# Dump rows stored one image sooner and three blocks long, block limits computed behind the last slots, class rows copied during the last block

## What is computed

```python
def reference(x, cls_tok, ...):
    h = tok_mixer(x)                       # exp(k)*v weighted by exp(w_bias), gate, out_w, layernorm
    h = concat([cls_tok, h], axis=1)       # the class token's row heads every image: 257 rows
    h = h + gated_recurrence(layernorm(h)) # W_r, W_i, W_in, scan over the sequence, W_out
    z = layernorm(h)
    shared = gelu(z @ Wfc_s + bfc_s) @ Wproj_s + bproj_s
    top2, gate = top_k(softmax(z @ Wr), 2) # gates normalised over the two
    routed = sum over e of gate_e * (gelu(z @ Wfc[e] + bfc[e]) @ Wproj[e] + bproj[e])
    return h + shared + routed             # (16, 257, 256)
```

## Time and profile before

| | |
|---|---|
| Median of three runs | 982.86 us |
| The profiled execution: time, span | 984.09 us, 982.0 us |
| PE busy | 921.2 us, 94% |
| DVE, ACT, POOL busy | 700.6, 482.3, 394.2 us |
| Mean granted TensorE clock | 0.98 of full |
| Moved by DMA | 89.11 MB, mean 91 GB/s |

### The profile page before, as it was taken

How to read it: one execution, slowest core, us unless ns; L and a number is a source line. 1 busy time by engine, 2 the same in 40 slices (tenths; PEclk the granted TensorE clock), 3 DMA queues, 4 the chain that set the end, 5 groups by cost and what they waited for, 6 DMA issues and landing times.

```text
span 982.0 us, 21456 instructions
## 1 busy us (share of the span) xinstructions
PE 921.2 (94%) x6825; PEld 858.8 (87%) x6825; DVE 700.6 (71%) x2093; ACT 482.3 (49%) x1146; POOL 394.2 (40%) x475
## 2 busy tenths in 40 slices
PE   7887999999999999999995999999999999999995
PEld 5665988888888888887985999999999999999995
DVE  3578788999999999999886464645646565654643
ACT  2123455555455555454341555555555555555553
POOL 6442233444333444315553334343533434342322
PEclk9898899999999999999997999999999999999998
DMA  9600001111101111101662728282642827473222
GB/s 257 187 22 23 30 31 50 54 54 54 46 18 43 54 54 54 54 1 40 199 220 69 220 44 220 43 221 43 161 107 44 219 44 190 77 205 60 44 43 33
DMA packets 50536, 89.11 MB, mean 91 GB/s; under 512 B 6733, under 2 KB 31199, under 8 KB 50498
## 3 DMA queue, kind: packets, MB, share of 16 engines
q0 software_dynamic: 31440, 58.52, 24.8%
q1 hardware_dynamic: 19058, 30.11, 10.8%
HBM read 59.28 MB, written 29.09 MB: 90 GB/s over the span
## 4 chain that ended last, share of the span: by engine, by line
PE 36%; DVE 27%; issue 23%; POOL 9%; ACT 3%; POOLq 1%; DVEq 1%; DMA 0%; ACTq 0%; SPq 0%
PE ps_nd L810 11%; PE ps_proj L794 5%; POOL out L755 5%; DVE rden L1996 4%; PE ps_ri L794 3%; DVE GL L1810 3%; PE ps_ip L960 3%; PE ps_ip L794 3%; PE ps_h L975 3%; DVE w2l L2228 2%; DVE st L1827 2%; PE ps_proj L889 1%; PE ps_proj L891 1%; PE ps_proj L894 1%; DVE h L1833 1%
## 5 line engine op out<-in xcount | busy, mean ns | idle before, releaser
L1810 DVE TENSOR_TENSOR GL<-g_act,GH 128x256 fp32r<-128x256 f32 (+1 forms) x416 | 174.6, 426 | 168.1 <-ACT GH L1440 152.9
L810 PE MATMUL ps_nd<-w2h,GH 128*128 128x256 f32 x832 | 242.5, 291 | 6.1 <-DVE Y L1999 4.8
L1435 ACT ACTIVATE g_act<-ps_proj,fcb 128x256 f32<-128x256 f32 (+1 forms) x272 | 129.1, 475 | 234.9 <-PE ps_proj L794 226.3
L810 PE MATMUL ps_nd<-w2h,GL 128*128 128x256 f32 x832 | 234.2, 281 | 0.0
L810 PE MATMUL ps_nd<-w2l,GH 128*128 128x256 f32 x832 | 233.3, 280 | 0.0
L810 PEld LDWEIGHTS ps_nd<-w2h,GH 128*128 128x128 f32 x832 | 156.6, 188 | 12.2 <-DVE Y L1999 5.0
L1440 ACT CAST GH<-g_act 128x256 fp32r<-128x256 f32 (+1 forms) x416 | 161.3, 400 | 1.2
L810 PEld LDWEIGHTS ps_nd<-w2l,GH 128*128 128x128 f32 x832 | 157.4, 189 | 0.0
L810 PEld LDWEIGHTS ps_nd<-w2h,GL 128*128 128x128 f32 x832 | 156.7, 188 | 0.0
L794 PE MATMUL ps_proj<-xh,w1h 128*128 128x256 f32 (+1 forms) x544 | 122.6, 307 | 12.6 <-DVE E L1989 8.9
L755 POOL DMA_INDIRECT out<-yb,rows_to x72 | 115.5, 1605 | 16.8 <-issue 13.2
(11 more groups left out here) (281 smaller groups left out, 1932.1 us busy)
## 6 DMA issues: line engine op xcount, KB each, us to landing
R<-v_rows SPq DMA_DIRECT2D x37, 260.0 KB
w1h<-fc_w POOLq DMA_DIRECT2D x9, 1024.0 KB
w2h<-pj_w POOLq DMA_DIRECT2D x9, 1024.0 KB
stage<-fc_w POOLq DMA_DIRECT2D x9, 1024.0 KB
stage<-pj_w POOLq DMA_DIRECT2D x9, 1024.0 KB
x<-x SPq DMA_DIRECT2D x28, 256.0 KB, 4.0
v_rows<-tail_rows SPq DMA_DIRECT2D x8, 520.0 KB
out<-yb SPq DMA_DIRECT2D x16, 256.0 KB
```

The source lines that it names most:

```text
L810: last = pe.matmul(banks[a], g[:, j, a * P:(a + 1) * P], w[i][:, j, :], start=(j == 0 and q == 0), stop=(j == HT - 1 and q == 2))
L1435: act.activation(g_act[:, j % G_SLOTS, 0:width], banks[j % len(banks)][:, 0:width], ACT.Gelu_apprx_tanh, bias=fcb[i][:, j:j + 1]).then_inc ...
L1810: dve.tensor_tensor(GL[:, j, 0:width], g_act[:, j % G_SLOTS, 0:width], GH[:, j, 0:width].bitcast(F32), ALU.subtract).then_inc(gl_done, 1)
```

## The change

- The counts for the tails are taken after image 13 (`NIMG - 3`), not 14, and the eight stores stand ahead of the base store of image 13 in SyncE's list. Each is three blocks long. POOL waits for them ahead of the scatters of image 14, not 15.
- The counting code of `experts_vector` is cut in two. `block_bounds`, up to `bounds_ready`, goes behind `slots_out(18, 0)`; `block_places`, up to `where_ready`, ahead of `base_sum(18, 0)`.
- SyncE copies the class rows when the adds of the last block but one have landed, and no longer waits for the last R. POOL waits for the last adds itself, as its last step.
- `next_low_first` and `next_low_second` become four calls of `next_low`; the instructions and their order stay.

```diff
                 for e in range(NE):
                     end = sp.value_load(ends_i[0:1, e:e + 1], min_val=e * LIST,
-                                        max_val=e * LIST + TOK - BLK)
-                    sp.dma_start(v_rows[bass.ds(end, 2 * BLK), :]
-                                 .rearrange("(b p a) m -> p b a m", b=2, a=2),
-                                 tail_rows[:].unsqueeze(1).to_broadcast([P, 2, 2, W])
+                                        max_val=e * LIST + TOK - 2 * BLK)
+                    sp.dma_start(v_rows[bass.ds(end, 3 * BLK), :]
+                                 .rearrange("(b p a) m -> p b a m", b=3, a=2),
+                                 tail_rows[:].unsqueeze(1).to_broadcast([P, 3, 2, W])
                                  ).then_inc(tails_stored, 16)
...
             base_out(16, 0)
+            tails(17, 1)
             base_out(17, 1)
-            tails(18, 0)
             base_out(18, 0)
...
-            sp.wait_ge(added, end * 32 + 32)
-            sp.wait_ge(rows_loaded, end * 16 + 16)
+            sp.wait_ge(added, end * 32)
             first_rows = out[0:NIMG * SEQ, :].rearrange("(n s) m -> n s m", s=SEQ)[:, 0, :]
...
-                    if isinstance(n, int) and n == NIMG - 1:
+                    if isinstance(n, int) and n == NIMG - 2:
                         pool.wait_ge(tails_stored, 16 * NE)
...
-            expert(NE, 0, *limits(NE), 0)
+            first, end = limits(NE)
+            expert(NE, 0, first, end, 0)
+            pool_wait(pool, added, end * 32 + 32).then_inc(carried, 1)
...
-                    if isinstance(n, int) and n == NIMG - 2:
-                        dve.wait_ge(run_ready, NIMG)
+                    if isinstance(n, int) and n == NIMG - 3:
+                        dve.wait_ge(run_ready, NIMG - 1)
                         dve.tensor_copy(ends_i[:], run[:]).then_inc(ends_ready, 1)
...
             slots_out(18, 0)
+            block_bounds(18, 0)
             low(18, 0, 1)
...
             v_norm(18, 0)
+            block_places(18, 0)
             base_sum(18, 0)
```

More of the change, by code:

```diff
@@ L668, in next_weights, with next_low @@
                 load_stage(pool, 1)
[L670 to L676, removed]
+            def next_low(t, par, q):
+                split_low(pool, 1, 1, q)
             def step(t, par):
@@ L735, in mixer_pool @@
             rstd_h(18, 0)
-            next_low_first(17, 1)
+            next_low(17, 1, 0)
+            next_low(17, 1, 1)
             rows_out(18, 0)
             affine(18, 0)
-            next_low_second(18, 0)
+            next_low(18, 0, 2)
+            next_low(18, 0, 3)
             rstd_u(18, 0)
@@ L2240, in constant, with count_chain, block_bounds, block_places @@
                 constants()
+            counted = [0]
+            def count_chain(instruction):
+                counted[0] += 1
+                instruction.then_inc(count_dve, 1)
+                dve.wait_ge(count_dve, counted[0])
+            def block_bounds(t, par):
+                chain = count_chain
+                dve.wait_ge(run_ready, NIMG + 1)
+                chain(dve.tensor_tensor(cnt["size"][:], run[:], list_f[:], ALU.subtract))
+                chain(dve.tensor_scalar(cnt_i[:], cnt["size"][:], float(BLK - 1), None, ALU.add))
+                chain(dve.tensor_scalar(cnt_s[:], cnt_i[:], BLK.bit_length() - 1, None,
+                                        ALU.arith_shift_right))
+                chain(dve.tensor_copy(cnt["n"][:], cnt_s[:]))
+                chain(dve.tensor_scalar(cnt["blocks"][:], cnt["n"][:], float(MIN_BLKS), None, ALU.max))
+                chain(dve.tensor_tensor_scan(cnt["end"][:], ones_pp[:, 0:NE], cnt["blocks"][:],
+                                             0.0, ALU.mult, ALU.add))
+                dve.memset(bounds[:, 0:1], 0)
+                dve.memset(lasts[:, 0:1], 0)
+                chain(dve.tensor_scalar(lasts[:, 1:NE + 1], cnt["end"][:], -1.0, None, ALU.add))
+                dve.tensor_copy(bounds[:, 1:NE + 1], cnt["end"][:]).then_inc(bounds_ready, 1)
+            def block_places(t, par):
+                chain = count_chain
+                dve.tensor_scalar(cnt["skip"][:], cnt["blocks"][:], -1.0, float(LIST_BLKS),
+                                  ALU.mult, ALU.add)
+                dve.tensor_copy(hop[:, NE - 1, :], block_f[:])
+                chain(dve.memset(carrier["count"][:], 0.0))
+                for e in range(NE - 1):
+                    last = dve.tensor_scalar(hop[:, e, :], block_f[:], cnt["end"][:, e:e + 1],
+                                             cnt["skip"][:, e:e + 1], ALU.is_ge, ALU.mult)
+                chain(last)
+                chain(dve.tensor_reduce(where[:], hop[:].rearrange("p e b -> p b e"), AX.X, ALU.add))
+                dve.tensor_copy(where_i[:], where[:]).then_inc(where_ready, 1)
             def cls_scan(t, par):
```

28 lines of the change are left out of this document (removed).

## The result

The changed kernel is slower. Its median is 988.94 us (986.83 to 991.55) against 982.83 (979.64 to 985.98) of the kernel before, eleven runs each: ratio 1.0059, 95% interval 1.0046 to 1.0073. The forecast was 981.3 with a range to 985.3. The profiled run is one of 988.94 us, span 987.3, clock 0.978. The profiled run of the kernel before, 984.09 us, lay 1.3 above its median, so the two traces show 4.9 us of the difference (5.3 on the span); the rest of the 6.1 between the medians stands in no trace.

The account below looks back on a forecast made before the run. TensorE was taken to set the pace except between mixer and experts (late residual sum, counts, limit loads) and at the end (class-row copy). Middle +0.3 and end -1.9 gave -1.6 us: 981.3 us, range 977.8 to 985.3.

Parts of the forecast that it names:

- The bytes of the tails: Dump-row stores before the last scatters: 6.39 MB, with 0.96 MB in their way, take 20.2 us and land at 512.4.
- the exchange of 3.3 against 3.1: DVE, image 14: base sum loses 3.3 us waiting for its store; the residual sum, no longer beside splits, returns 3.1.
- The first hold: Mixer's end: a GL part due at 517.9 is caught by POOL's first pair of splits until 522.6.
- The end, -1.9: Program end: copying class rows during the last block ends the span at about 980.1 instead of 982.0, 1.9 us less.
- a tail like that of now, 0.4: Program end: after POOL sees the last add and a 0.2 us operation, only 0.4 us remain.
- The bound of 0: Program end: no gain if the end of the program waits for something other than the class-row copy.
- the rest of the chain follow as it did: Mixer's end: behind the caught GL part, 9.7 us as before, so TensorE ends at 532.3.
- the middle: Passage from mixer to experts: half way between +0.3 and +1.8, less 0.7 for the clock, gives +0.3 us.
- The 3.5 us of limit loads: Ahead of the transposes: TensorE loads limits for 3.5 us after its mixer work, reaching 534.4 or 535.8.
- Clock: TensorE around the passage: staying at full clock saves up to 2.2 us, falling earlier costs up to 2; counted at -0.7.
- an idle stretch of 4.2 us: TensorE in the passage: its clock falls to half 4.2 us behind its last matmul.
- rival (c): Mixer's end: TensorE idles over 6 us, the clock falls during its last products, 984 to 987.8 us; chance 0.17.

Follow-up runs that it names:

- a_nosplit: Changed kernel with POOL's four splits for the first routed expert replaced by memsets to zero: 983.86 us, ratio 0.9988 to the kernel before.
- b_bounds: Kernel before with only the counting code moved (block_bounds behind the last slots, block_places ahead of the last base sum): 982.17 us, ratio 0.9979.
- b_tails: Kernel before with only the tails edit (one image sooner, three blocks long): 988.0 us, ratio 1.0035.
- b_nosplit: Kernel before with POOL's four splits for the first routed expert replaced by memsets to zero: 981.22 us, ratio 0.9963.
- a_bounds_late: Changed kernel with block_bounds moved directly ahead of block_places, behind the last GL part: 988.0 us, ratio 1.0028 to the kernel before.

## Why the prediction was wrong

**Right.** The bytes of the tails and the time they take: POOL got on at 512.07 where 512.7 was worked out, and the engines moved 366 to 376 GB/s meanwhile. All later POOL times came within 0.7 us, and R was asked for at 528.81 (529.5). The base sum of image 14 waited for the store behind the tails and L2219 fell back to 0.69 us, as the exchange of 3.3 against 3.1 had it; the slots came at 516.16 (516.3). The first hold ended at 522.12 (522.6), though on another instruction than the one named, so that this agreement is partly luck.

**The end, -1.9: wrong by 3.7 us on the span, some 3.2 in the time.** The step was "a tail like that of now, 0.4". I read POOL's and SyncE's last working rows and not the drains behind them. The bound of 0 that the prediction gave ("if the end of the program waits for something else") was not wide enough either: its POOL wait made it +1.8 on the span. The two runs without that wait show that the copy was worth nothing (0.9999) and that the wait cost 2 us.

**What was held, and how often.** The prediction put the hold on a GL part. It fell on `c_blocks`, a step of the moved code itself, since I had looked for holds only among operations with two SBUF inputs. The Trainium skill (SBUF — State Buffer, "SBUF: two separate sides") names VectorE operations in a two-port mode beside them, and gives a copy from SBUF to SBUF in float32 as one; this small one-input float32 operation (5.23 us) fits that. Two inputs were not even the condition beside memsets: in a_nosplit a GL part begun at 522.96 took its usual 0.43 us inside the second pair (522.82 to 524.68), while the one-input `c_skip` behind it, begun at 523.31, took 1.40. For the first pair this changed little, since the GL part behind it was as late as forecast. But the prediction then let "the rest of the chain follow as it did", to 532.3, though its own second pair, ending at 532.4, had to start at 527.7, just where the last GL part was due. That part took 5.23 us instead of 0.43. This is the step that failed in the middle: the path behind the first hold was taken to meet no second one. Of the 4.8 us TensorE felt 2.42, its idle time, as it had products queued until 529.9.

**The 3.5 us of limit loads: charged, though they cost nothing.** The prediction let them stand behind TensorE's last matmul. The trace after has them beside its last matmuls:

```profile
L1414 PEldq TENSOR_LOAD <-bounds x8: 296/307/572, 534.2 to 539.2; - x8
```

They begin at 534.2, when the class row's products (533.33 to 537.67) are still running, and the transposes, which stand behind the first five loads, follow at once. In the earlier trace rows they began at 530.6, behind idle time, because the limits came late. Limits in time cost nothing, so the gain is not a shift of 3.5 us but their removal, in b_bounds as here.

**Clock.** Counted at -0.7, between -2.2 and +2. The class row's 24 products took 4.34 us; at full clock, in the run with the limits alone (b_bounds, TensorE, the first and the last of the 24), they follow one another at (526.44 - 523.82)/23 = 0.114 us, 2.7 for all:

```profile
523.82 0.28 PE L1402 MATMUL ps_h<-w2h,GH 128*2 128x256 f32 x1
...
526.44 0.28 PE L1402 MATMUL ps_h<-w2h,GL 128*2 128x256 f32 x1
```

That is 1.6 us for the second idle stretch alone, and more for the first. The gain behind the mixer did not come either: the clock was down again at 540, and the first twelve expert products took 2.82 us against 2.93. The prediction's condition for a fall, an idle stretch of 4.2 us, was one case only: here the clock fell 3.1 us behind the last matmul once, and once behind a stretch of 2.42. So rival (c), 984 to 987.8, had the mechanism: an idle stretch over 6 us, the clock down during the mixer's last products. It fell short by the end and by the second hold.

**Not in the prediction:** v_norm of image 15 waits 1.16 us for the scatters of image 13, whose buffer it reuses (DVE's first row above); that their data lies in the same DMA engines as the tails is the likely reason, which no run tests. TensorE is idle 1.52 us there, 0.66 in the kernel before. It costs nothing in the end, since what follows waits for the base store and for the end of the splits, and the slots of image 15 came no later than forecast.

In sum, the middle was forecast at +0.3 and came out at +3.6 on the span. TensorE's end of the mixer, put half way between 530.9 and 532.3, came at 537.67, 6.1 us later. Of that, 0.7 is that the path to 532.3 was the one that came, 2.42 the idle time before the held part's products, 1.6 the class row at the lower clock, and most of the remaining 1.4 the products from 523.14 to 526.5 at the lower clock. Against these 6.1 stand the loads (-3.5), and the clock's forecast gain (0.7) is missing: 6.1 - 3.5 + 0.7 = 3.3, the whole error. The end was forecast at -1.9 and came out at +1.8 on the span. The loss of 5.8 us thus hangs on the tails edit, which moves the splits onto VectorE's chain and lets the clock fall (3.4 us by b_tails), and on the end (2.1 by the run with DVE's wait). The third of the three, the limits, is good by itself and gains nothing in this company.

## What to carry to other kernels

When an edit moves a long GpSimd operation, list every VectorE instruction that could stand beside it, small ones with one input too, and ask for each pair anew, not for the first alone; the cost is what stands behind the held one, not its size. Before an end is shortened, read the closing drain of each engine: the second latest sets what there is to gain. And measure the parts of a change one by one, since here one of three gave 2.1 us alone, and its gain was gone only beside another.

## What the runs showed of the hardware

- `c_blocks`, a VectorE operation on 128x8 elements that took 0.17 us by itself, took 5.23 us beside two GpSimd operations of 2.3 us each, and 2.62 us beside two memsets (1.85 us for both, b_nosplit). VectorE got nothing between the two in any trace that was read. A GL part, which reads two SBUF tensors, was not held inside a pair of memsets (0.43 us from 522.96, the memsets from 522.82 to 524.68, a_nosplit).
- A held instruction can begin before the GpSimd row that holds it: 0.08 us in b_tails (520.53 against 520.61), 0.55 in the changed kernel (516.89 against 517.44), 0.66 in a_bounds_late (522.84 against 523.50), 0.73 in a_nosplit (515.19 against 515.92). In each of them POOL was still in the scatter before. Spans on POOL are rough, so whether the row or the hold starts elsewhere stays open.
- GpSimd's closing drain ended 4.3 to 4.4 us behind the issue of its last indirect DMA when it was reached early, and took 3.75 us when it was reached after that DMA had landed.
- TensorE's register loads ran beside its queued matmuls: the loads of limits began at 534.2, and the five that the transposes stand behind cost nothing, as the transposes began at 537.65, where the 24 products ended.
- TensorE's granted clock fell to half 4.2 us behind the last matmul in the kernel before and 3.1 us behind it in the changed one, and once while TensorE was busy again, 1.2 us after an idle stretch of 2.42 us (532.35 to about 533.5).
- Kernels whose last wait is POOL's have 1.6 us around their span; those that end on SyncE or DVE have 2.1. No run here tells why.
